# A second attention: the first batch's queries, arranged by TensorE products with 0/1 matrices instead of a trip through DRAM

## The reference

```
x = x + attention_0(layernorm(x), ctx, ctx)
x = x + moe_0(layernorm(x))            # x @ W_in, top 2 of 8 experts, @ W_out
q = layernorm(x) @ Wq + bq             # 16 heads of 16
k, v = ctx @ Wk + bk, ctx @ Wv + bv
x = x + softmax(q k^T / 4) v @ Wo + bo
x = x + moe_1(x)                       # top 1 of 8 experts
```

## Time and profile before

| | |
|---|---|
| median of 3 runs | 1040.02 us (1030.73 to 1041.53) |
| profiled execution, its own time | 1039.32 us |
| its span in the profile | 1037.5 us |
| busy share of TensorE, VectorE, ScalarE, GpSimd | 89%, 70%, 44%, 22% |
| mean granted TensorE clock | 0.93 of full speed |

### The profile page before, as it was taken

How to read it: one execution, slowest core, us unless ns; L and a number is a source line. 1 busy time by engine, 2 the same in 40 slices (tenths; PEclk the granted TensorE clock), 3 DMA queues, 4 the chain that set the end, 5 groups by cost and what they waited for, 6 DMA issues and landing times.

```text
span 1037.5 us, 19986 instructions
## 1 busy us (share of the span) xinstructions
PE 928.1 (89%) x6612; PEld 581.9 (56%) x6612; DVE 726.1 (70%) x1958; ACT 457.5 (44%) x1020; POOL 223.1 (22%) x198
## 2 busy tenths in 40 slices
PE   5989999898988899999999878899999887887995
PEld 3656666565745677887886543333434343334774
DVE  5482858677688767666665457879788886754895
ACT  5344543332323543433432321367666655642332
POOL 0304303101012244344321001110010011104573
PEclk9989999898996999999999997899999887686998
DMA  9633020004347311111111666454272007334241
GB/s 288 216 122 122 1 82 1 21 11 126 107 140 237 113 52 50 47 52 49 47 49 60 191 131 164 52 95 70 68 124 56 21 21 203 123 122 121 84 127 32
DMA packets 70112, 98.52 MB, mean 95 GB/s; under 512 B 8732, under 2 KB 57119, under 8 KB 67584
## 3 DMA queue, kind: packets, MB, share of 16 engines
q1 hardware_dynamic: 59872, 61.54, 21.4%
q0 software_dynamic: 10144, 35.69, 12.6%
HBM read 70.91 MB, written 27.02 MB: 94 GB/s over the span
## 4 chain that ended last, share of the span: by engine, by line
PE 68%; DVE 20%; ACT 5%; DMA 3%; issue 2%; SPq 0%; POOLq 0%; POOL 0%; ACTq 0%; DVEq 0%
PE pb L1054 13%; PE pb L1074 8%; PE pb L1177 5%; PE pb L887 4%; PE pb L1075 4%; PE pb L1199 4%; PE pb L811 3%; PE pb L840 3%; PE pb L876 3%; PE pb L896 3%; PE pb L853 3%; PE pb L817 3%; DVE MX L2089 2%; PE pb L1155 2%; ACT EX L1501 2%
## 5 line engine op out<-in xcount | busy, mean ns | idle before, releaser
L1436 ACT ACTIVATE m<-pb,b1m 128x128 f32<-128x128 f32 x404 | 115.6, 369 | 158.8 <-PE pb L1054 158.7
L1501 ACT ACTIVATE EX<-pb 128x512 f32<-128x512 f32 x256 | 136.8, 601 | 92.7 <-PE pb L1199 91.8
L2089 DVE TENSOR_REDUCE MX<-pb 128x1 f32<-128x512 f32 x256 | 159.3, 682 | 22.9 <-PE pb L1155 22.3
L1054 PE MATMUL pb<-xt,w1h 128*128 128x128 f16 x1616 | 156.3, 221 | 2.9 <-DVE xt L1965 1.5
L1074 PE MATMUL pb<-w,mh 128*128 x404 | 149.3, 379 | 3.8 <-DVE ml L1975 3.6
L1054 PEld LDWEIGHTS pb<-xt,w1h 128*128 x1616 | 120.2, 99 | 40.0 <-issue 4.1
L1054 PE MATMUL pb<-xt,w1l 128*128 128x128 f16 x808 | 112.1, 221 | 0.0
L811 PE MATMUL pb<-identh 128*128 128x512 f16 x371 | 98.9, 410 | 14.3 <-DVE identh L1612 8.1
L1075 PE MATMUL pb<-w,ml 128*128 x404 | 110.1, 273 | 0.0
L1199 PE MATMUL pb<-QS,KS 49*128 49x512 f32 x256 | 80.9, 527 | 11.2 <-ACT EX L1501 9.7
L1199 PEld LDWEIGHTS pb<-QS,KS 49*128 49x128 f32 x256 | 32.1, 199 | 86.7 <-issue 61.4
(11 more groups left out here) (322 smaller groups left out, 1506.2 us busy)
## 6 DMA issues: line engine op xcount, KB each, us to landing
SR<-in_w1m SPq DMA_DIRECT2D x20, 512.0 KB, 5.6
SR<-in_w2m SPq DMA_DIRECT2D x12, 512.0 KB, 5.0
KS<-kd SPq DMA_DIRECT2D x48, 128.0 KB, 5.5
QS<-qd POOLq DMA_DIRECT2D x18, 256.0 KB, 9.1
kd<-KHL POOLq DMA_DIRECT2D x8, 512.0 KB, 6.3
vd<-VAB POOLq DMA_DIRECT2D x4, 1024.0 KB, 4.4
rows<-HL POOLq DMA_DIRECT2D x8, 512.0 KB, 4.1
GB<-outs SPq DMA_DIRECT2D x8, 512.0 KB, 7.8
```

Source lines behind the costliest of these rows:

```text
L1054: ins = pe.matmul(k.ap[:, h4 * TOK:(h4 + 1) * TOK], wt[:, bass.ds(regs[j], 128)], M.xt[j % 2][:, xc, :], start=i == 0, stop=i == 5)
L1436: ins = act.activation(M.m32[x % 2][:, h4, :], k.ap[:, h4 * TOK:(h4 + 1) * TOK], M.func, bias=M.b1[:, bass.ds(reg + 4 * g + h4, 1)], scale ...
L1501: act.activation(EX[m % len(EX)][:, i, :], k.ap, ACT.Exp, scale=0.25).then_inc(k.out, 1)
L2089: v.tensor_reduce(mx[:, t, 2 * s + j:2 * s + j + 1], k.ap, AX.X, ALU.max).then_inc(k.out, 1)
```

## The change

For batch 0 alone, SyncE's two stores, six loads and their waits go, and `first_loaded` with them. In their place VectorE builds, at the start of `wg_norm`, two 0/1 matrices `selq0` and `selq1` of [128, 4, 128] from the identity: the first puts the high part into groups 0 and 1 of each row block, the second the low part into group 2, all else is zero. Once both halves of QHL are ready, TensorE multiplies each by them, two products accumulated for each of the 8 slices of QS, into banks of the ring `psum_m`; ScalarE copies the even slices into QS, VectorE the odd ones. `maxima(0)` waits for these banks instead of the loads. Batches 1 to 3 keep their way. Line numbers differ between the two kernels; in the rows below, L803, L809, L888 and L1107 of the changed kernel are L811, L817, L896 and L1114 of the one before.

```diff
+        sel = [nc.alloc_sbuf_tensor_at(f"selq{i}", [128, 4, 128], F32R, offset=MZ.start + (16 + 2 * i) * K) for i in range(2)]
...
-            p["first_loaded"]()
             weave(p["load_v"](0))
...
@@ SyncE, qprep @@
                     w.wait_ge(*M.take().ev)
-                    load(f"qw{c}", qd[b].rearrange("q p c n -> p q c n")[:, :, c, :], QHL[c][:, :, :].bitcast(F32))
-                    if b == 0 and c == 1:
-                        for cc in range(2):
-                            w.wait_ge(sem(f"d_qw{cc}"), 16)
-                        sv = qd[0].rearrange("q (j r b) c n -> j q r (b c) n", j=2, r=16)
-                        for j in range(2):
-                            for g, x in enumerate((0, 0, 1)):
-                                r0 = 64 * j + 16 * g
-                                load("qsf", QS[0][r0:r0 + 16, :, :].bitcast(F32), sv[j, x])
+                    if b:
+                        load(f"qw{c}", qd[b].rearrange("q p c n -> p q c n")[:, :, c, :], QHL[c][:, :, :].bitcast(F32))
                     yield from pause(GAP)
+                if b == 0:
+                    M.skip(8)
+                    yield from pause(4)
...
@@ TensorE, qprep, behind the projections @@
+                if b == 0:
+                    for s in range(8):
+                        hb, c = divmod(s, 2)
+                        w.wait_ge(sem("selq"), 1)
+                        w.wait_ge(*ks[c].ev)
+                        k = psum_m.take()
+                        w.wait_ge(*k.before)
+                        for i in range(2):
+                            ins = pe.matmul(k.ap, sel[i][:, hb, :], QHL[c][:, i, :], start=i == 0, stop=i == 1)
+                        ins.then_inc(k.full, 1)
+                        q0.append(k)
+                        if s % 2:
+                            yield
...
@@ TensorE, maxima @@
-                    w.wait_ge(*q_loaded(b))
+                    if b:
+                        w.wait_ge(*q_loaded(b))
+                    else:
+                        for k in q0[4 * half:4 * half + 4]:
+                            w.wait_ge(*k.ev)
...
@@ ScalarE, qprep (VectorE copies the odd slices with tensor_copy) @@
+                if b == 0:
+                    for s in range(8):
+                        k = psum_m.take()
+                        q0.append(k)
+                        if s % 2:
+                            yield
+                        else:
+                            w.wait_ge(*k.mm)
+                            act.activation(QS[0][:, s, :], k.ap, ACT.Copy).then_inc(k.out, 1)
...
@@ VectorE @@
             def wg_norm():
+                for x in sel:
+                    v.memset(x[:, :, :].bitcast(F32), 0.0).then_inc(*c.up("v"))
+                w.wait_ge(*c.last)
+                cols = ident[:, :].rearrange("p (j r b) -> p b j r", j=2, r=16)
+                at = [x[:, :, :].rearrange("p b (j g r) -> p b j g r", j=2, g=4) for x in sel]
+                for i, g in ((0, 0), (0, 1), (1, 2)):
+                    ins = v.tensor_copy(at[i][:, :, :, g, :], cols)
+                ins.then_inc(*c.up("selq"))
                 w.wait_ge(sem("d_we"), 2 * 16)
                 v.tensor_tensor(wgt[:, 0:16], wg8[:, :], wg8[:, :], ALU.mult).then_inc(*c.up("v"))
```

More of the change, by code:

```diff
@@ L793, in sync_program @@
                        mlp=lambda b: pause(13), kv=kv, split=split, moe_pre=lambda b: pause(MP + 9), tables=nop, gate_weights=nop,
-                       route=nop, experts=experts, combine_begin=nop, combine=combine, first_loaded=first_loaded, clear=clear, norms=nop, qprep=qprep,
+                       route=nop, experts=experts, combine_begin=nop, combine=combine, clear=clear, norms=nop, qprep=qprep,
                        load_v=load_v, maxima=maxima, attend_loads=attend_loads, attend=attend, gate_rows=lambda b: pause(12), wg_norm=nop, gate=gate,
@@ L897, in project @@
                 ins.then_inc(k.full, 1)
+                return k
             def kv(b):
@@ L1117, in combine @@
                         yield
+            q0 = []
             def qprep(b):
@@ L1280, in tensor_program @@
             order(dict(start=nop, kv_load=nop, loads1=nop, loads2=nop, pre=pre, s_exp=s_exp, rest=rest, mlp=mlp, kv=kv, split=skip_split,
-                       moe_pre=moe_pre, tables=tables, gate_weights=gate_weights, route=route, experts=experts, combine_begin=nop, combine=combine, first_loaded=nop, clear=nop, norms=nop, qprep=qprep,
+                       moe_pre=moe_pre, tables=tables, gate_weights=gate_weights, route=route, experts=experts, combine_begin=nop, combine=combine, clear=nop, norms=nop, qprep=qprep,
                        load_v=lambda b: pause(1), maxima=maxima, attend_loads=nop, attend=attend, gate_rows=lambda b: pause(12), wg_norm=wg_norm, gate=gate,
@@ L1460, in combine @@
                 yield from pause(2)
+            q0 = []
             def qprep(b):
                 w.wait_ge(sem("ln3"), 2 if b else 1)
-                w.wait_ge(sem("d_qw1"), 16 * b)
+                if b > 1:
+                    w.wait_ge(sem("d_qw1"), 16 * (b - 1))
                 at = 4 * (b - 1) if b else 0
@@ L1476, in qprep @@
                     w.wait_ge(*k.mm)
-                    w.wait_ge(sem(f"d_qw{c}"), 16 * b)
+                    if b == 1:
+                        w.wait_ge(*q0[-1].mm)
+                    elif b:
+                        w.wait_ge(sem(f"d_qw{c}"), 16 * (b - 1))
                     act.activation(QHL[c][:, 0, :], k.ap[:, 0:S], ACT.Identity, bias=pp[:, 12 + c:13 + c]).then_inc(sem("q_hi"), 1)
                     yield from pause(GAP)
+                if b == 0:
[7 more added lines that the diff above has]
+                            act.activation(QS[0][:, s, :], k.ap, ACT.Copy).then_inc(k.out, 1)
             def maxima(b):
@@ L1555, in scalar_program @@
             order(dict(start=nop, kv_load=nop, loads1=nop, loads2=nop, pre=pre, s_exp=s_exp, rest=rest, mlp=mlp, kv=kv, split=split,
-                       moe_pre=moe_pre, tables=tables, gate_weights=lambda: Y.skip(1), route=route, experts=experts, combine_begin=nop, combine=combine, first_loaded=nop, clear=nop, norms=nop, qprep=qprep,
+                       moe_pre=moe_pre, tables=tables, gate_weights=lambda: Y.skip(1), route=route, experts=experts, combine_begin=nop, combine=combine, clear=nop, norms=nop, qprep=qprep,
                        load_v=lambda b: pause(1), maxima=maxima, attend_loads=nop, attend=attend, gate_rows=lambda b: pause(12), wg_norm=wg_norm, gate=gate,
@@ L2064, in qprep @@
                     w.wait_ge(sem("q_hi"), 2 * b + cc + 1)
[L2065 removed]
+                    if b > 1:
+                        w.wait_ge(sem(f"d_qw{cc}"), 16 * (b - 1))
                     v.scalar_tensor_tensor(out=QHL[cc][:, 1, :], in0=k.ap[:, 0:S], scalar=pp[:, 12 + cc:13 + cc], in1=QHL[cc][:, 0, :].bitcast(F32),
@@ L2068, in qprep @@
                     yield from pause(GAP)
+                if b == 0:
+                    for s in range(8):
+                        k = psum_m.take()
+                        if s % 2:
+                            w.wait_ge(*k.mm)
+                            v.tensor_copy(QS[0][:, s, :], k.ap).then_inc(k.out, 1)
+                            yield
             def rows_out(b, half):
@@ L2207, in vector_program @@
                        moe_pre=moe_pre, tables=tables, gate_weights=gate_weights, route=route, experts=experts,
-                       combine_begin=combine_begin, combine=combine, first_loaded=nop, clear=nop, norms=norms, qprep=qprep,
+                       combine_begin=combine_begin, combine=combine, clear=nop, norms=norms, qprep=qprep,
                        load_v=lambda b: pause(1), maxima=maxima, attend_loads=nop, attend=attend, gate_rows=gate_rows, wg_norm=wg_norm, gate=gate,
@@ L2340, in qprep @@
                 yield from pause(2 * GAP)
+                if b == 0:
+                    yield from pause(4)
+                    return
                 for c in range(2):
-                    w.wait_ge(sem(f"d_qw{c}"), 16 * (b + 1))
+                    w.wait_ge(sem(f"d_qw{c}"), 16 * b)
                 if b == 2:
@@ L2368, in pool_program @@
                        moe_pre=moe_pre, tables=lambda: Y.skip(1), gate_weights=lambda: Y.skip(1), route=lambda r: Y.skip(2) if r is R0 else None, experts=experts,
-                       combine_begin=nop, combine=lambda b: pause(6), first_loaded=nop, clear=nop, norms=nop, qprep=qprep,
+                       combine_begin=nop, combine=lambda b: pause(6), clear=nop, norms=nop, qprep=qprep,
                        load_v=lambda b: pause(1), maxima=lambda b: pause(64 + (b == NB - 1)), attend_loads=nop, attend=attend, gate_rows=lambda b: pause(12), wg_norm=nop, gate=gate,
```

16 lines of the change are left out of this document (6 added, 10 removed).

## The result

| | before | after |
|---|---|---|
| median, run in turns on one chip, 10 runs each | 1036.94 us (1030.73 to 1042.18) | 1046.60 us (1037.62 to 1049.73) |
| profiled execution, its span, mean granted clock | 1039.32, 1037.5 us, 0.928 | 1037.62, 1035.7 us, 0.940 |

The ratio is 1.0092, interval [1.006, 1.0125]: the change costs about 0.9%, 9.5 us, where +4.7 us was forecast. The two profiled executions can't be subtracted: that of after is one of its two lowest, and has the higher clock. For this first comparison, where none is left out, the means are 1036.83 and 1045.52, +8.7 us.

A forecast was written before the change was run, and what follows sets the result against it. The prediction took the chain of waits, with TensorE 68% busy, as the bound. Removed transfers at 0, matrices +1.1 and products +3.6 gave +4.7 us: 1044.0, or 1044.7 us against the median, range 1035 to 1052.

The forecast's parts named there:

- +1.1 and +3.6: Delays in us: TensorE's wait at the router product for the matrices, and the 16 products ahead of the third batch's transposes.
- The matrices: VectorE's memsets and copies ahead of the router-weight chain: 1.6 us there, making TensorE wait 1.1 us, passed on undiminished.
- A product costs 0.23 us: Each of the 16 query products on TensorE takes 0.23 us, lower bound 0.22, upper bounds 0.43 and 0.86.
- rivals 1 and 2: A query product costs 0.43 us, total 1047.2 us, chance 0.17; or 0.86 us like plain fp32, total 1053.3, chance 0.04.
- The eight dummies are on the path: Eight dummies, 1.75 us, run after the query products and directly before the third batch's transposes, which move to 606.4.
- The copies hide: The eight copies of slices by VectorE and ScalarE end by 605.6 and 604.8, before the transposes at 606.4.
- The trip through DRAM is worth 0: Removing two stores, six loads and their waits gains 0 us, hidden behind the combine and VectorE's norms.
- Rival 3, a kinder clock: The half-clock stretch after the norms comes out at full clock, gaining some 6 us: 1038.7 us, chance 0.13.
- 1039.3 + 4.7 = 1044.0: The summed delay of 4.7 us added in full to the profiled execution's time; 1044.7 us against the median.
- Rival 4: The clock is less kind by the same 6 us: +10.7 us, 1050.7 us, chance 0.08.

The follow-up runs named there:

- again: The changed kernel without any edit, run on a second chip beside the kernel before: 1066.49 us, ratio 1.0074.
- again_2: The changed kernel without any edit, run on a third chip beside the kernel before: 1064.62 us, ratio 1.0136.
- build_late: The changed kernel with the 0/1 matrices built behind the router weights, in combine_begin, not at the start of wg_norm: ratio 1.0072 against the kernel before.
- twice: The changed kernel with four products per slice in place of two, 32 in all: 1062.29 us, ratio 1.0102 against the kernel before.
- no_fill: The changed kernel without the eight dummies ahead of the third batch's transposes: ratio 1.0026 against the kernel before.
- early_loads: The kernel before without first_loaded, so VA and batch 1's keys are issued straight behind the QS loads: 1056.95 us, ratio 1.0018.
- norms_early: The kernel before with the layer-norm sums of batches 1 and 2 taken within the combine, in VectorE's waits for output products: 1048.10 us, ratio 0.9967.
- build_only: The kernel before with the two 0/1 matrices built in wg_norm but never read: ratio 0.9961.
- shift_dummies: The kernel before with 30 more dummies, 6 ahead of the router transpose and 24 behind the second query projection: 1061.11 us, ratio 1.0072.
- after_norms_early: The changed kernel with the layer-norm sums of batches 1 and 2 taken within the combine: 1059.86 us, ratio 1.008 against the kernel before.
- before_again: The kernel before, unchanged, run against itself for a second trace: 1055.73 us, ratio 1.0015.

## Why the prediction was right or wrong

**Right: direction, class and every term read in the trace.** Within 1% was forecast at 0.83, and 1046.6 lies in the range. The forecast was +1.1 and +3.6; the trace of the profiled execution, `again` and `again_2` show 1.26 and 3.56 to 3.64.

- *The matrices.* Forecast 1.6 us on VectorE and a wait of 1.1 on TensorE: 1.75 and 1.10, with 1.26 in the stage. `build_late` shows it as a matter of place alone.
- *A product costs 0.23 us.* From one row pair of L1155 and L1199 at 49 rows. Fourteen take 3.64 us (3.48 from the first's start to the dummies behind them, 0.25 each, with one short wait of 0.3 us for a copy), and the fourteen that `twice` adds cost 0.214 each. The upper bounds of 0.43 and 0.86 (rivals 1 and 2) fell. On the single line view:

```profile
L1135 PE MATMUL pb<-QHL,selq x16: 387/396/796, 592.8 to 598.2; 128*128 128x512 f32 x16
```

  one record for a product, 396 ns in the median, against two of 592 ns for a product of L896. The Trainium skill (FP8 and Floating Point Precision, section TensorE Precision Notes) says that the reduced form of fp32 is truncated to FP22 and that true fp32 takes four passes. The trace agrees with one pass for the reduced form, over 128 rows too: its record of 396 ns is near the fp16 dummy's 379.
- *The eight dummies are on the path.* `no_fill` takes 1.75 us away.
- *The copies hide.* They do: in the changed kernel a weight load waits 0.3 us for one, and in `twice` no wait for one is left.
- *The trip through DRAM is worth 0.* `early_loads` and `norms_early` show it from two sides.
- *Rival 3, a kinder clock*, did not come: the idle stretch of 4.44 us and the 0.50 behind it are there, as its "against" said. The stage behind came out 1.3 us shorter, so the clock there was a little kinder, and in `build_only` and `twice` by 3.2 and 3.4 us, of the 6 the rival had.

**Wrong: the size, by a factor of two.** The step that failed is the one from the sum to the time, "1039.3 + 4.7 = 1044.0": it lets a delay on the path pass to the end at its own price. The measured price is +8.7 to +8.8 us. Rival 4, "the clock is less kind", had the number (+10.7) but I gave it 0.08 and hung it on one stretch. The runs show in its place:
1. 2.0 us that go with a mean clock lower by 0.0026. A pure delay has 1.2 us that go so, and the half-clock W_out products (1.7 us, in one of the changed kernel's three traces and in that of `shift_dummies`) are one place where it is seen. As the clock gives back 1.3 us behind the norms, other stages would have to lose 3.3; which ones is not shown. Nor is it why a shift by 4.8 us should meet the clock's steps worse in all: the shift of `build_only` met them better, its trace 3.2 us shorter behind the norms.
2. 2.0 ± 1.2 us at equal clock that no stage of the traces holds. `shift_dummies` has none of it (4.9 for 4.84), the changed kernel and `build_late` have; but the difference between changed kernel and `shift_dummies` is 1.9 ± 1.9 us, the fit's slope is one number for stages of unlike sensitivity, and `build_only` misses its own term of 1.27 by 2.4 the other way (-1.1 ± 1.4). This stays open. No run here takes it apart, and it is not put down to the copies or to early transfers, of which the second was tried alone and cost 0.1 ± 1.4.

## What to carry to other kernels

Before a transfer is replaced, look at what ends last behind it: here VectorE's norms hid the whole trip, its removal was worth nothing, and moving eight small operations of those norms into idle time took 2.6 us of waiting away, and the kernel with it was the quickest measured. Work that an engine's order places behind waits and ahead of dummies is paid in full; give it the dummies' places. And a sum of terms forecasts the trace, to 0.2 us here, but the time of a kernel with several half-clock stretches only to some 5 us, so a change of 0.5% needs the mean of many runs and their clocks, and not one profile beside another. Compare two traces stage by stage, and past the stage of the change too: a term there can be offset by a shorter half-clock stretch behind it, as in `build_only` and `twice`.

## What the runs showed of the hardware

- **Half clock while products run.** In `build_late` TensorE fell to 0.51 over 608 to 611.5 with its products running; the sixteen took 5.41 us for 3.72. Its longest wait in the 15 us before was 1.23 us, as in the changed kernel's trace, where the same products ran at 1.0.
- **The same wait, half clock of unlike length.** Behind a wait of 4.45 us the 0.50 lasted 12 us (before), 9 (changed) and 4 (`build_only`, `twice`), and behind one of 1.83 us 3 (`norms_early`).
- **A long step.** In a later stage some traces have a clock of 0.72 over 800 to 860 (`early_loads`, `build_late`, `after_norms_early`) where others have 0.86 and 0.91 (before, after). Two traces of the kernel before have 0.86 and 0.80, three of the changed one 0.91, 0.89 and 0.96; no program was traced both at 0.72 and above it. The first of the three:

```profile
800.00:860.00 60.00, 55.38 (x280) 21.77 (x280) 45.14 (x116) 32.08 (x63) 2.95 (x2) 0.72 0.06 19
```

- **The last expert stage is about 16 us longer in all traces of the experiments' three chips**, that of the unchanged kernel too (1054.4 us of span for 1037.5): the copies of xt take 82.7 us from the first to the last (81.2 to 84.0 in the twelve traces) where they take 65.7 in the traces of before and after. VectorE waits there for something that the profile calls remote, which those two do not show at all (waits of `before_again` from 930 on):

```profile
DVE xt L1965 <- remote: 18.7, 6, 4.8
```

  What it is stays open. These 16 us are most of the difference between the 1055 to 1058 us of these chips and the 1037 of the first comparison, and they come without the change as with it.
- **Prices.** A memset of 128x512 is 0.5 us on VectorE; a copy of 128x512 out of PSUM 0.69 us on VectorE, 0.58 to 0.60 on ScalarE; a weight load for the products 0.19 us, beside the product before.
